# Sinkhorn's turning products as one of 128 stationary columns in place of four of 32

## The chip, the cores and the metric

One core of a Trainium2 chip runs the whole program. The metric is the device time of one execution in microseconds (us), as the median of several executions. The engines are TensorE (PE; PEld is its weight load), VectorE (DVE), ScalarE (ACT), GpSimd (POOL) and SyncE (SP), which issues DMAs.

## What is computed

Two layers over x (128 batches, 32 rows, 128 features). Layer 0 scales x by Sinkhorn's iteration and sends it through a routed feed-forward net; layer 1 is a GRU over the rows, then attention and a mixture of experts. The change lies in the first part alone:

```python
K = jnp.exp(-M / MU)
K = K / jnp.maximum(K.sum(axis=(-2, -1), keepdims=True), EPS)
u, v = r[..., None], 0
for _ in range(31):        # frozen once u has stopped moving
    v = c / jnp.maximum(jnp.einsum('bnm,bnk->bmk', K, u), EPS)
    u = r / jnp.maximum(jnp.einsum('bnm,bmk->bnk', K, v), EPS)
P = u * K * jnp.swapaxes(v, -2, -1)
```

K is 128 matrices of 32 x 128, u is one column of 32 and v one of 128 for each batch.

## The kernel before

`sinkhorn` keeps K in buf_a with the rows (n) of four batches on the partitions, and K transposed in buf_b with the features (m) on the partitions, already scaled by c. The 128 batches are cut into four groups h = 0 to 3 of 32 batches, so that the engines can work on different groups at the same time. Each group has a PSUM bank of its own, ps_g[h].

A round of the iteration has these steps for a group, each named after its function or operation:

- `to_columns(h)` (TensorE, L235): K times u. u stands block-diagonally in u_pad, 32 stationary columns a product. Eight products of 128 x 32 stationary and 128 moving columns, four to each of two accumulations; product j writes partitions 32j to 32j+31 of ps_v.
- den_v (ScalarE, L211): copies the 128 x 128 result from PSUM, with a bias that keeps it above zero.
- `turn(h)` (TensorE, L241): den_v has the features along its free axis. Products with den_v as the stationary operand and the 0/1 matrix `pick` (32 columns) as the moving one pick the wanted entries and put the features on the partitions. Four products, product q with columns 32q to 32q+31 of den_v, into partitions 32q to 32q+31 of ps_g[h], columns 256 to 287.
- `invert(h)` (VectorE, L329): the reciprocal, written block-diagonally to v_pad.
- `to_rows(h)` (TensorE, L249): K transposed times v, eight products like those of `to_columns`, into ps_u.
- `turn_back(h)` (L333), `inverse(h)` (L338) and `spread(h)` (L344) on VectorE: a transpose in blocks of 32, the reciprocal, and the next u_pad.

GpSimd keeps a history of u (L186 to L194), and ScalarE judges how far u has moved and keeps a history of v (L213 to L219). After the 31 rounds the history of the round at which the iteration would have stopped is read back.

The order on each engine is written out by hand in `one_round`; semaphores carry the rest. On TensorE it is: columns 0, columns 1, columns 2, turn 0, turn 1, columns 3, turn 2, rows 0, turn 3, rows 1, rows 2, rows 3. A turn waits for its den_v (semaphore v_den), rows wait for `invert` (v_ready), columns for `spread` of the round before (u_ready). TensorE's first round stands by itself, since there the rows also wait for the scaling of buf_b by c (L324); the other 30 run in a loop, two to a pass. SyncE fetches the weights of the next stages during the first rounds.

Every fp32 product is recorded as two passes, each with a weight load of its own.

Of the kernel before, what the change touches and what calls it, by code (L numbers as in the profile page):

```python
# [12 lines left out]
B, N, D = 128, 32, 128  # L13
# [47 lines left out]
def sinkhorn(nc, io, consts, K, KT, u_last, v_last, early, x_n):  # L61

    ident, ones = consts.ident, consts.ones
    NG, W, BW = GROUPS_S, T // GROUPS_S, TG * BG
    WIDE = 36
    with ExitStack() as ctx:
# [7 lines left out]
        pick = mem.sb("pick", [P, BG, BG, TI])  # L74
# [10 lines left out]
        den_v = mem.sb("den_v", [P, NG, D])  # L85
# [8 lines left out]
        stop = mem.sb("stop", [1, 1])  # L94
        stop_i = mem.sb("stop_i", [1, 1], I32)
        moved = mem.sb("moved", [P, ITERS, NG])
        ps_g = [mem.ps(f"ps_g{k}", [P, 512]) for k in range(NG)]
# [8 lines left out]
        v_mm, v_den, t_mm, v_ready, u_mm, turned, inv_done, u_kept = (  # L106
            mem.sem("s_" + n) for n in ("v_mm", "v_den", "t_mm", "v_ready", "u_mm", "turned", "inv_done", "u_kept"))
# [15 lines left out]
        with nc.Block() as block:  # L123

            @block.sync
            def _(sp):
                sp.dma_start(r_t[:], io["r_t"]).then_inc(s["cr_in"], 16)
                sp.dma_start(c_t[:], io["cond_t"]).then_inc(s["cr_in"], 16)
                for h in range(NG):
                    sp.dma_start(Kv[:, h * TG:(h + 1) * TG, :], xv[:, h * TG:(h + 1) * TG, :]).then_inc(x_in[h], 16)  # L130
                for h in range(NG):
                    sp.dma_start(of_group(KT[:], h), of_group(io["x_t"], h)).then_inc(xt_in[h], 16)

                sp.wait_ge(u_mm, 2 * NG)
                sp.dma_start(early.wx[:], io["gru_wx"].rearrange("(g p) d -> p g d", p=P)).then_inc(early.gru_in, 16)
                sp.dma_start(early.wh[:], io["gru_wh"].rearrange("(g p) d -> p g d", p=P)).then_inc(early.gru_in, 16)
                sp.dma_start(early.wp[:], io["gru_wp"]).then_inc(early.gru_in, 16)
                sp.dma_start(early.bias[:], io["gru_b"]).then_inc(early.gru_in, 16)
                sp.dma_start(early.h_in[:], io["cond_t"]).then_inc(early.gru_in, 16)
                sp.dma_start(early.up[:], io["up0_t"]).then_inc(early.ffn_in, 16)  # L140
                sp.dma_start(early.down[:], io["down0_t"].rearrange("(j p) d -> p j d", p=P)).then_inc(early.ffn_in, 16)
                sp.dma_start(x_n[:], io["x_nt"]).then_inc(early.ffn_in, 16)
                sp.dma_start(early.gate_w[:], io["gate_w0_t"]).then_inc(early.gate_in, 16)
                sp.dma_start(early.gate_b[:], io["gate_b0"].broadcast_to([P, 8])).then_inc(early.gate_in, 16)
# [77 lines left out]
            @block.tensor  # L222
            def _(pe):
                mm = nc.tensor.matmul
                pe.wait_ge(s["made"], 17)
                pe.wait_ge(s["ksums"], NG)
                mm(ps_s[:, 0:G], same_batch[:], ksum[:], start=True, stop=True).then_inc(s["sums_mm"], 1)
                pe.wait_ge(s["kinv_out"], 1)
                mm(ps_s[:, G:G + B], ones[:], kinv_row[:].rearrange("p c t -> p (c t)"), start=True, stop=True).then_inc(s["kinv_mm"], 1)

                def to_columns(h):
                    for i in range(TI):
                        for j in range(BG):
                            t = h * TG + j * TI + i
                            last = mm(ps_v[h][32 * j:32 * j + 32, :], u_pad[:, h, j, 32 * i:32 * i + 32], K[:, t * D:(t + 1) * D],  # L235
                                      start=i == 0, stop=i == TI - 1)
                    last.then_inc(v_mm, 1)

                def turn(h):
                    for q in range(4):  # L240
                        last = mm(ps_g[h][32 * q:32 * q + 32, 2 * D:2 * D + BW], den_v[:, h, 32 * q:32 * q + 32],  # L241
                                  pick[:].rearrange("p c j i -> p (c j i)"), start=True, stop=True)
                    last.then_inc(t_mm, 1)

                def to_rows(h):
                    for i in range(TI):
                        for c in range(BG):
                            b = c * G + h * TG + i * BG
                            last = mm(ps_u[h][32 * c:32 * c + 32, :], v_pad[:, h, c, 32 * i:32 * i + 32], KT[:, b * N:(b + BG) * N],  # L249
                                      start=i == 0, stop=i == TI - 1)  # L250
                    last.then_inc(u_mm, 1)

                def one_round(i, first):
                    pe.wait_ge(u_ready[0], i + 1)
                    to_columns(0)
                    pe.wait_ge(u_ready[1], i + 1)
                    to_columns(1)
                    pe.wait_ge(u_ready[2], i + 1)
                    to_columns(2)
                    pe.wait_ge(v_den, i + 1)  # L260
                    turn(0)
                    pe.wait_ge(v_den, i + 2)
                    turn(1)
                    pe.wait_ge(u_ready[3], i + 1)
                    to_columns(3)
                    pe.wait_ge(v_den, i + 3)
                    turn(2)
                    pe.wait_ge(v_ready, i + 1)
                    if first:
                        pe.wait_ge(s["kt_scaled"], 1)  # L270
                    to_rows(0)
                    pe.wait_ge(v_den, i + 4)
                    turn(3)
                    pe.wait_ge(v_ready, i + 2)
                    if first:
                        pe.wait_ge(s["kt_scaled"], 2)
                    to_rows(1)
                    pe.wait_ge(v_ready, i + 3)
                    if first:
                        pe.wait_ge(s["kt_scaled"], 3)  # L280
                    to_rows(2)
                    pe.wait_ge(v_ready, i + 4)
                    if first:
                        pe.wait_ge(s["kt_scaled"], 4)
                    to_rows(3)

                one_round(0, True)
                with nc.tensor.Fori(NG, NG * ITERS, 2 * NG) as i:
                    one_round(i, False)
                    one_round(i + NG, False)  # L290
# [1676 lines left out]
```

## Time and profile before

| | us |
|---|---|
| median of 3 runs (548.59 to 551.55) | 549.93 |
| the profiled execution's own time | 553.06 |
| its span in the trace | 551.3 |
| TensorE busy | 480.2 |
| VectorE busy | 371.9 |
| ScalarE busy | 319.2 |
| GpSimd busy | 182.3 |

The durations below come from the one profiled execution, which took 3.13 us more than the median. Sinkhorn runs from 16.8 to about 151 us of the span. The duration of a pass as shown is a latency with a modelled end: passes overlap, so the pace is read from where one group starts and where the next does. A start time is counted from the start of the span.

### The profile page before, as it was taken

The page shows a single profiled execution, that of the slowest core. Times are in us where ns is not written, and L with a number is a line of the kernel's source. Part 1 is how long each engine was busy: PE and PEld are TensorE (multiplying, and loading weights), DVE is VectorE, ACT ScalarE, POOL GpSimd, SP SyncE. Part 2 cuts the span into 40 slices and gives each one's busy share as a digit, 9 for nine tenths or more (in the row PEclk, how much of TensorE's full clock was granted, in tenths as well). Part 3 has the DMA queues.
Part 4 walks back from the last instruction along what each step waited for, and adds up shares of the span by engine and source line. Part 5 has one row for each costly group of instructions (what it writes and reads, how often), then busy time and mean ns, then how long its engine had stood idle before and what let it go on. Part 6 is the DMA issues. An engine that isn't in the chain of part 4 may idle for free. (4 is left out here: it accounts for less than half of the span.)

```text
span 551.3 us, 23767 instructions
## 1 busy us (share of the span) xinstructions
PE 480.2 (87%) x8992; PEld 395.2 (72%) x8992; DVE 371.9 (67%) x1329; ACT 319.2 (58%) x784; POOL 182.3 (33%) x445
## 2 busy tenths in 40 slices
PE   0799999999969989999999797799999840999994
PEld 0589999999847446666666595588888730999994
DVE  4778878878877656666575457368999875355552
ACT  4555555555546925564554535487888730777772
POOL 3244444444400000000000077223567663354553
PEclk9999999999979999999999977599999985999998
DMA  9261000000000367833300020000011122333330
GB/s 243 69 204 47 0 0 0 0 0 0 0 1 2 81 157 201 257 78 77 96 1 1 1 81 1 2 2 2 28 53 41 63 94 81 87 108 104 110 101 19
DMA packets 24190, 34.37 MB, mean 62 GB/s; under 512 B 3616, under 2 KB 17957, under 8 KB 23752
## 3 DMA queue, kind: packets, MB, share of 16 engines
q1 hardware_dynamic: 21360, 27.23, 17.9%
q0 software_dynamic: 2784, 6.56, 3.4%
q8 instruction: 25, 0.41, 0.3%
q14 instruction: 21, 0.17, 0.1%
HBM read 25.98 MB, written 8.26 MB: 62 GB/s over the span
## 5 line engine op out<-in xcount | busy, mean ns | idle before, releaser
L211 ACT ACTIVATE den_v<-ps_g,floor 128x128 f32<-128x128 f32 x124 | 45.5, 368 | 45.3 <-PE ps_g L235 41.3
L249 PE MATMUL ps_g<-buf_b,v_pad 128*32 128x128 f32 x1984 | 66.9, 274 | 1.9 <-DVE v_pad L329 1.4
L235 PE MATMUL ps_g<-buf_a,u_pad 128*32 128x128 f32 x1984 | 67.8, 278 | 0.3
L235 PEld LDWEIGHTS ps_g<-buf_a,u_pad 128*32 128x32 f32 x1984 | 53.8, 112 | 1.8 <-DVE u_pad L344 1.1
L1031 POOL MEMSET eps<- 128x1 f32 x1 | 0.1, 98 | 164.5 <-POOLq L572 164.5
L1773 POOL DMA_INDIRECT out<-yb,token_i x39 | 38.5, 987 | 47.7 <-DVE resid L1875 46.5
L249 PEld LDWEIGHTS ps_g<-buf_b,v_pad 128*32 128x32 f32 x1984 | 50.6, 110 | 2.8 <-DVE v_pad L329 2.1
L639 PE MATMUL ps_h<-buf_c,up 128*128 128x512 f32 x96 | 49.9, 616 | 0.3
L329 DVE RECIPROCAL v_pad<-ps_g 128x32 f32<-128x32 f32 x124 | 38.9, 334 | 14.0 <-PE ps_g L241 11.6
L1343 POOL TENSOR_TENSOR vb<-vn,row_mask 128x1024 f32<-128x1024 f32 x16 | 30.2, 1890 | 44.8 <-PE ps_o L1422 23.8
L1796 PE MATMUL m_h<-xT,w_near 128*128 128x128 f32 x312 | 42.4, 280 | 0.0
L1806 PE MATMUL m_y<-w,hid_t 128*128 x312 | 41.3, 275 | 0.1
L333 DVE STREAM_TRANSPOSE den_u<-ps_g 128x128 f32<-128x128 f32 x124 | 37.9, 306 | 4.0 <-PE ps_g L249 0.3
L193 POOL TENSOR_SCALAR held_u<-inv_u 128x8 f32<-128x8 f32 x124 | 24.3, 196 | 45.3 <-DVE inv_u L338 44.5
L1796 PEld LDWEIGHTS m_h<-xT,w_near 128*128 128x128 f32 x312 | 39.0, 196 | 0.2 <-ACT xT L1836 0.2
L1806 PEld LDWEIGHTS m_y<-w,hid_t 128*128 128x128 f32 x312 | 38.0, 192 | 0.3 <-issue 0.3
L1891 DVE TENSOR_TENSOR yb<-m_y,resid 128x128 f32<-128x128 f32 x39 | 11.4, 292 | 37.7 <-PE m_y L1806 37.7
L1336 POOL DMA_INDIRECT sorted_x<-rows,slot_i x32 | 31.4, 981 | 11.1 <-issue 7.9
L766 ACT ACTIVATE relu<-ps_h 128x512 f32<-128x512 f32 x48 | 28.2, 588 | 11.1 <-PE ps_h L639 11.1
L194 POOL TENSOR_TENSOR u_hist<-held_u,r_t 128x8 f32 x124 | 25.3, 204 | 22.4 <-POOL held_u L193 22.4
L241 PE MATMUL ps_g<-pick,den_v 128*32 128x32 f32 x992 | 31.3, 201 | 0.0
L649 PE MATMUL ps_y<-act,down 128*128 128x512 f32 x64 | 31.3, 593 | 0.0
(316 smaller groups left out, 1159.9 us busy)
## 6 DMA issues: line engine op xcount, KB each, us to landing
cw_b<-cw_d SPq DMA_DIRECT2D x16, 512.0 KB, 7.9
xt<-sorted_x SPq DMA_DIRECT2D x39, 136.0 KB, 2.2
w<-in_w SPq DMA_DIRECT2D x2, 2048.0 KB, 16.2
buf_a<-in_x SPq DMA_DIRECT2D x4, 512.0 KB, 6.6
buf_b<-in_x_t SPq DMA_DIRECT2D x4, 512.0 KB, 7.2
buf_d<-in_x_nt SPq DMA_DIRECT2D x1, 2048.0 KB, 8.8
sorted_x<-nobody SPq DMA_DIRECT2D x1, 1088.0 KB, 5.3
out<-yb,token_i POOLq DMA_INDIRECT x39, 2.5
```

What stands on the lines that cost most here:

```text
L211: fn(den_v[:, h, :], ps_v[h], ACT.Relu, bias=floor[:]).then_inc(v_den, 1)
L235: last = mm(ps_v[h][32 * j:32 * j + 32, :], u_pad[:, h, j, 32 * i:32 * i + 32], K[:, t * D:(t + 1) * D], start=i == 0, stop=i == TI - 1)
L241: last = mm(ps_g[h][32 * q:32 * q + 32, 2 * D:2 * D + BW], den_v[:, h, 32 * q:32 * q + 32], pick[:].rearrange("p c j i -> p (c j i)"), sta ...
L249: last = mm(ps_u[h][32 * c:32 * c + 32, :], v_pad[:, h, c, 32 * i:32 * i + 32], KT[:, b * N:(b + BG) * N], start=i == 0, stop=i == TI - 1)
L329: v.reciprocal(diagonal_v(h), ps_t[h]).then_inc(v_ready, 1)
L333: v.transpose(den_u[:, h, 0:D], ps_u[h]).then_inc(turned, 1)
L639: mm(ps_h[p % 2][:], up[:, j * P:(j + 1) * P], pt_n[:, q * W:(q + 1) * W], start=True, stop=True).then_inc(h_mm, 1)
L649: mm(ps_y[q % 2][:], down[:, ORDER[k], :], held(p), start=k == 0, stop=k == J - 1).then_inc(y_mm, 1)
L1336: g.indirect_dma_start(sorted_x, bass.IndirectOffsetOnAxis(ap=tables.slot_i[:, t:t + 1], axis=0), rows[:, t, :], None).then_inc(tables.sen ...
L1773: nc.gpsimd.indirect_dma_start(out, bass.IndirectOffsetOnAxis(ap=token_i[:, d:d + 1], axis=0), yb[:, k, :], None, bounds_check=T - 1, oob_ ...
L1796: last = mm(ps_h[d % 2][:, q * P:(q + 1) * P], w1_near[:, d % NEAR, q * P:(q + 1) * P], x_t[:, d % 2, :], start=True, stop=True)
L1806: last = mm(ps_y[d % 2][:, 0:D], hid_t[:, d % 2, q, :], w2[:, bass.ds(at + q * D, D)], start=q == 0, stop=q == Q - 1)
```

## The change

The four products of `turn` become one, whose stationary operand is the whole of den_v for the group (128 columns) and whose output is all 128 partitions. What is computed, the moving operand and the semaphore that the last product raises stay the same, as does everything else in the kernel.

```diff
                 def turn(h):
-                    for q in range(4):
-                        last = mm(ps_g[h][32 * q:32 * q + 32, 2 * D:2 * D + BW], den_v[:, h, 32 * q:32 * q + 32],
-                                  pick[:].rearrange("p c j i -> p (c j i)"), start=True, stop=True)
-                    last.then_inc(t_mm, 1)
+                    mm(ps_g[h][:, 2 * D:2 * D + BW], den_v[:, h, :], pick[:].rearrange("p c j i -> p (c j i)"),
+                       start=True, stop=True).then_inc(t_mm, 1)
```

## Rows read from the trace of the kernel before

**Rows 1.** The page: busy time of each engine, and TensorE's clock in 40 slices.

```profile
PE 480.2 (87%) x8992; PEld 395.2 (72%) x8992; DVE 371.9 (67%) x1329; ACT 319.2 (58%) x784; POOL 182.3 (33%) x445
...
PEclk9999999999979999999999977599999985999998
```

**Rows 2.** The page's costliest groups: busy us, mean ns, idle before and its releaser.

```profile
L249 PE MATMUL ps_g<-buf_b,v_pad 128*32 128x128 f32 x1984 | 66.9, 274 | 1.9 <-DVE v_pad L329 1.4
L235 PE MATMUL ps_g<-buf_a,u_pad 128*32 128x128 f32 x1984 | 67.8, 278 | 0.3
...
L241 PE MATMUL ps_g<-pick,den_v 128*32 128x32 f32 x992 | 31.3, 201 | 0.0
```

**Rows 3.** Timeline of TensorE's matmuls, one round: start us, length us, engine, line.

```profile
121.63 1.49 PE L235 MATMUL ps_g<-buf_a,u_pad 128*32 128x128 f32 x48
122.94 0.50 PE L241 MATMUL ps_g<-pick,den_v 128*32 128x32 f32 x16
123.26 0.62 PE L235 MATMUL ps_g<-buf_a,u_pad 128*32 128x128 f32 x16
123.70 0.24 PE L241 MATMUL ps_g<-pick,den_v 128*32 128x32 f32 x8
123.78 0.64 PE L249 MATMUL ps_g<-buf_b,v_pad 128*32 128x128 f32 x16
124.37 0.27 PE L241 MATMUL ps_g<-pick,den_v 128*32 128x32 f32 x8
124.45 1.50 PE L249 MATMUL ps_g<-buf_b,v_pad 128*32 128x128 f32 x48
125.77 0.40 PE L235 MATMUL ps_g<-buf_a,u_pad 128*32 128x128 f32 x8
```

**Rows 4.** Timeline of weight loads and ScalarE in the same round.

```profile
123.17 0.16 PEld L241 LDWEIGHTS ps_g<-pick,den_v 128*32 128x32 f32 x8
123.23 0.16 PEld L235 LDWEIGHTS ps_g<-buf_a,u_pad 128*32 128x32 f32 x8
...
124.37 0.16 PEld L241 LDWEIGHTS ps_g<-pick,den_v 128*32 128x32 f32 x8 [0.21 <-ACT den_v L211]
...
123.95 0.37 ACT L211 ACTIVATE den_v<-ps_g,floor 128x128 f32<-128x128 f32 x1 [0.39 <-PE ps_g L235]
```

**Rows 5.** Timeline of weight loads, 164.3 to 165.3 us, the feed-forward net's gate.

```profile
164.34 0.97 PEld L624 LDWEIGHTS ps_gz<-gate_w,buf_c 128*128 128x128 f32 x8
165.23 0.19 PEld L639 LDWEIGHTS ps_h<-buf_c,up 128*128 128x128 f32 x1
```

**Rows 6.** Timeline of weight loads, 442.7 to 445.3 us, attention.

```profile
443.95 0.30 PEld L1443 LDWEIGHTS ps_pt<-w_proj,o_t 128*128 128x128 f32 x2
444.17 0.31 PEld L1445 LDWEIGHTS ps_pt<-rows,ident 128*128 128x128 f32 x2
```

**Rows 7.** Timeline of matmuls, the same stretch of attention.

```profile
443.08 0.24 PE L1455 MATMUL ps_ss<-hot,every 128*128 128x32 bf16 x4
443.25 0.77 PE L1422 MATMUL ps_o<-vb,prob_t 128*32 128x36 f32 x64
```

**Rows 8.** Timeline of matmuls, 365.1 to 366.0 us, attention.

```profile
365.41 0.40 PE L1443 MATMUL ps_pt<-w_proj,o_t 128*128 128x136 f32 x2
365.64 0.40 PE L1445 MATMUL ps_pt<-rows,ident 128*128 x2
365.96 0.24 PE L1422 MATMUL ps_o<-vb,prob_t 128*32 128x36 f32 x4
```

**Rows 9.** Timeline of matmuls, end of the first round and start of the second.

```profile
24.19 0.65 PE L249 MATMUL ps_g<-buf_b,v_pad 128*32 128x128 f32 x16 [0.69 <-DVE v_pad L329]
24.90 2.17 PE L235 MATMUL ps_g<-buf_a,u_pad 128*32 128x128 f32 x48
```

**Rows 10.** Busy time of the engines in windows; the column before DMA is TensorE's clock.

```profile
300.00:350.00 50.00, 38.78 (x222) 33.37 (x230) 26.37 (x107) 25.03 (x54) 20.82 (x55) 0.81 0.07 23
...
400.00:450.00 50.00, 44.03 (x1252) 37.80 (x1251) 44.57 (x158) 36.78 (x88) 32.85 (x28) 1.00 0.16 57
```

## The prediction, made before the changed kernel was built

> **What bounds the kernel now.** I read the page's busy lines first: TensorE is busy 87% of the span, and the clock line stands at 9 (full) through slices 2 to 11, in which Sinkhorn runs [rows 1]. The costliest groups give the size of the stage: L235 and L249 have 1984 pass records each and L241, the line that the change touches, 992 [rows 2]. Over 31 rounds that is 64, 64 and 32 passes a round: 32 products of columns, 32 of rows and 16 of turning, since an fp32 product is two passes here.
>
> Then the timeline of TensorE over one round [rows 3]. Take 121.63 as zero: columns of groups 0 to 2 from 0, turn(0) at 1.31, columns of group 3 at 1.63, turn(2) at 2.07, rows of group 0 at 2.15, turn(3) at 2.74, rows of groups 1 to 3 at 2.82, next round at 4.14. Two things are to be seen. First, 48 passes take 1.31 us both times (121.63 to 122.94, 124.45 to 125.77): 27 ns each on average, which is one set of four passes in 0.109 us. The four products of a set go to four different 32-column strips and run beside one another. A round has 32 such sets, 32 x 0.109 = 3.49 us of its 4.14. Second, the remaining 0.65 us lies around the turns. Turn(1)'s first weight load starts at 123.17 and the weights of the next columns are loading at 123.23 [rows 4]; turn(3)'s starts at 124.37, with 0.21 us of idle load path ahead of it that ScalarE's den_v ended [rows 4]. The last set of columns(1) begins at 7 x 0.109 = 0.76, and turn(1) at 1.54: 0.78 later. The last set of columns(3) begins at 1.96, and turn(3) at 2.74: again 0.78. So the round's critical path is: columns 0 and 1, eviction by ScalarE, **turn(1)**, columns 3, eviction, **turn(3)**, rows 1 to 3. Each of those two turns costs 0.09 us on it (123.17 to 123.26, 124.37 to 124.45). Turn(0) and turn(2) lie in slack: 1.54 - 1.31 = 0.23 us before turn(1) may start, and 2.74 less the end of rows(0), which is 2.15 + 0.02 + 4 x 0.109 = 2.61, so 0.13 us. ScalarE is not the limit, its den_v takes 0.37 us four times a round [rows 4].
>
> **What the change removes.** Per turn, four products (eight passes, eight weight loads) become one (two and two): 24 passes less a round, 744 less in all. But the eight passes of today are two sets of four that run together, and a turn with its weights loaded ahead is over in 0.08 us (turn(2): 123.70, then rows(0) at 123.78 [rows 3]). What is removed is worth at most 0.09 us a turn.
>
> **What it adds, 1: wide weight loads.** A load of 32 columns becomes one of 128. Rows for that: eight loads of 128 fp32 columns at L624, whose products stream only 8 columns, start at 164.34, and the next group's at 165.23: 0.89 / 8 = 0.111 us each [rows 5]. Nothing hides in it: the load alone sets the pace. With no load ahead, L1443's two loads start at 443.95 and the next at 444.17 [rows 6]: 0.22 us until the second pass can stream. A turn is therefore 0.22 us of loads and then 32 columns, 0.027 us by the set's 0.109 for 128. Bounds: 0.11 if the first load were hidden, 0.22 if not; den_v or the switch below lies ahead of every turn but turn(1), and turn(1)'s first load can at best begin when turn(0)'s second has ended, so I take 0.22 for each.
>
> **What it adds, 2: a change of layout.** L235 and L249 use 32-column strips, the new turn the whole width. The kernel has this alternation in its attention stage. Whole to strips: L1455's four passes (8 columns, 0.24 us with the last's modelled tail of 0.166) start the last pass at 443.15, and the strips of L1422 begin at 443.25 [rows 6, 7]: 0.09 after its stream. Pairs of passes start every 0.23 us there (365.41, 365.64), so L1445's has streamed at 365.87; L1422 begins at 365.96 [rows 8]: 0.09. Strips to whole: L1422's 64 passes end, as modelled, at 444.02, each lasting 0.200, so the last starts at 443.82 and streams 36 columns (0.03); L1443's load starts at 443.95 [rows 6, 7]: 0.10. Where the layout stays, nothing of this is seen: L241 starts at 122.94, when the twelve sets before it are through [rows 3]. So a switch costs 0.09 us each way, with nothing streamed or loaded in it. A round gets three excursions (turn(0) with turn(1), turn(2), turn(3)), six switches. The bounds are 0 and 0.10; I take 0.09, as two of the three places have it.
>
> The Trainium skill speaks here against the change ("TensorEngine Tiling (Array Packing)", section Key Properties): changing the tiling mode, not just the tile, drains TensorE. It gives no time; the trace agrees, with 0.09 us. Without that rule the sum would be the 560 us of the second case below.
>
> **The new round**, from 0: columns 0 to 2 end at 1.31; switch, 1.40; turn(0)'s loads, 1.62; turn(1)'s den_v was ready at 1.54, its loads end at 1.84; it streams, 1.87; switch, 1.96; four sets, the first 0.024 longer as after a wait today (123.78 to 124.37 includes it), end 2.42, the last begun at 2.31; switch, 2.51; turn(2), 2.76; switch, 2.86; rows(0) end at 3.31; den_v(3) was ready at 2.31 + 0.78 = 3.09; switch, 3.41; turn(3), 3.66; switch, 3.75; twelve sets and 0.024, 5.08. **The round goes from 4.14 to 5.08 us.** As a check, all of it on TensorE: 3.49 + 4 x 0.22 + 3 x 0.027 + 6 x 0.09 + 3 x 0.024 = 5.07. No wait is left on the path. VectorE's reciprocal for rows(0) is due at 1.62 + 0.81 = 2.43 (today turn(0)'s last set starts 0.03 behind 122.94, and rows(0) 0.81 later, at 123.78), before 2.86; its spread for the next round keeps its 0.1 us of slack behind rows(0) and (1), which move as a block with turn(3).
>
> Rounds: 30 after the first. The second is longer today by its slow start (48 passes take 2.17 us as against 1.49 [rows 3, 9]), which is no wait at the turns, so it takes the cost in full like the rest: 30 x 0.945 = 28.4 us. The first is paced by the scaling of KT on VectorE (waits of 0.69 us for the reciprocal behind it [rows 9]); it takes between 0 and 0.9, I say 0.2. Everything behind Sinkhorn moves back as it is; its DMAs are landed long before. SP and POOL queues are passed by nothing. The sum against the profiled execution's own 553.06 us is 581.7; the median of the three runs is 3.1 lower, 549.93, so the forecast is **578.5 us**. This case's own range: 570 (the three switches into the turns hidden under the loads, 3 x 0.09 x 30 = 8.1 less) to 586 (0.13 for every switch, start to start as at L1443, instead of 0.09: 7.2 more).
>
> **Rivals.** (a) Loads, but no switch cost, because both layouts here use all 128 rows. For it: nothing in Sinkhorn's own rows shows a switch. Against: the three places above, two of them from the whole width to exactly this strip. Then turn(0)'s first load hides; turn(1) runs from 1.54 to 1.79, columns(3) start 0.16 late, turn(3) goes from 2.90 to 3.15, the round is 4.46: 30 x 0.32 = 9.7, so **560 us**. (b) The other side: TensorE is bound by how many passes it can issue. 160 passes in 4.14 us are 25.9 ns each; 24 fewer would save 0.62 us a round, 18.6 in all, so **531 us**. It decides if a wide pass costs one issue slot like a narrow one. Against: the passes of a set of four start together and the next set waits 0.109 us, which is the streaming of 128 columns; and L624's wide passes are 0.111 apart with 8 columns. The Trainium skill ("TensorE: Matmul & The Clock Gate", section Wait — 56ns, not 53.3ns?) states a floor of about 25 ns from start to start, however few columns; by that rule this rival would hold, and the average looks like it, but L624's pace does not follow it. (c) Both loads hide and no switch costs: the two turns on the path stream 2 x 0.027 instead of 0.09, 30 x 2 x 0.03 = 2 us less, **548 us**, no change. Against: den_v is what they load, and it is only just written. (d) TensorE's granted clock falls in Sinkhorn, as it does in 300 to 350 us (0.81) [rows 10], since six pauses a round are new. Against: 400 to 450 us, with the same alternation, has 1.00. A tenth of the stage at half clock costs some 15 us: **594 us**.
>
> **How the numbers follow.** Forecast case 0.80, (a) 0.09, (b) 0.03, (c) 0.03, (d) 0.05. The forecast case's own range leaves out more than 2 in 10 with the other cases, so the range reaches down to (a): 559 to 587. A measurement tells about 0.5% (2.7 us) from no change. Faster by more: (b), 0.03. Within it: (c), 0.03. Slower: 0.94.
>
> **What would show it.** Right, if in the profile after: L241 has 248 passes, its second load 0.11 after its first; between the last set of columns(2) and turn(0)'s load 0.2 us pass from start to start (0.109 and 0.09); from turn to next strips 0.12; a steady round of 5.08; ScalarE's den_v no longer ends a wait of L241; clock still 1.00. Wrong, if strips load while the wide product streams (a), if wide loads are 0.03 apart (b), or if the clock line drops below 9 in slices 2 to 12 (d).

## The result and the profile after

The changed kernel takes 578.6 us (median of 4 runs, 578.2 to 580.89) and the kernel before, on the same chip, 550.74 us (4 runs, 548.59 to 554.19): a ratio of 1.0508, with a 95% interval of 1.0445 to 1.0571. It is slower, by 27.9 us in the medians. The profiled executions are 25.1 us apart (553.06 and 578.2 us).

The page's busy lines and costliest groups of the kernel after, in the columns of [rows 1, 2]:

```profile
span 576.5 us, 22279 instructions
PE 507.1 (88%) x8248; PEld 410.6 (71%) x8248; DVE 374.5 (65%) x1329; ACT 318.7 (55%) x784; POOL 182.3 (32%) x445
...
PEclk9999999999998999999999997799999995799998
...
L247 PE MATMUL ps_g<-buf_b,v_pad 128*32 128x128 f32 x1984 | 67.4, 276 | 1.2 <-DVE v_pad L327 1.2
L235 PE MATMUL ps_g<-buf_a,u_pad 128*32 128x128 f32 x1984 | 67.9, 278 | 0.3
...
L240 PEld LDWEIGHTS ps_g<-pick,den_v 128*128 128x128 f32 x248 | 34.6, 189 | 18.5 <-issue 18.0
...
L240 PE MATMUL ps_g<-pick,den_v 128*128 128x32 f32 x248 | 44.9, 284 | 0.0
```

TensorE has 744 passes less (8992 to 8248) and is busy for 27 us longer. The turn's passes are down from 992 to 248, and yet their group is busy for 44.9 us where it was for 31.3 [rows 2]. The new entry is at the end of the load's line: the load path stood idle for 18.0 us ahead of L240, and what ended it is "issue", that is, nothing that the profile knows of. The line's own view counts them, beside what is left of the old wait:

```profile
L240 PEld LDWEIGHTS ps_g<-pick,den_v x248: 186/189/192, 18.6 to 177.6; 128*128 128x128 f32 x124
...
  issue: 18.0, 91
  ACT den_v L211: 0.5, 2
```

91 + 2 are three excursions a round in 31 rounds (an excursion is one stay in the wide layout between stretches of strips: turn(0) with turn(1), turn(2), turn(3)), of 0.2 us each: about half of it while the last set still streams, the rest with nothing in it. The wait for ScalarE's den_v ahead of turn(3), 0.21 us of idle load path in a round of before [rows 4], is gone: TensorE now comes later than den_v at all excursions but two.

One steady round, in the timeline of TensorE's matmuls (the columns of [rows 3]):

```profile
122.56 1.49 PE L235 MATMUL ps_g<-buf_a,u_pad 128*32 128x128 f32 x48
123.98 0.63 PE L240 MATMUL ps_g<-pick,den_v 128*128 128x32 f32 x4
124.55 0.64 PE L235 MATMUL ps_g<-buf_a,u_pad 128*32 128x128 f32 x16
125.12 0.41 PE L240 MATMUL ps_g<-pick,den_v 128*128 128x32 f32 x2
125.46 0.64 PE L247 MATMUL ps_g<-buf_b,v_pad 128*32 128x128 f32 x16
126.03 0.41 PE L240 MATMUL ps_g<-pick,den_v 128*128 128x32 f32 x2
126.37 1.52 PE L247 MATMUL ps_g<-buf_b,v_pad 128*32 128x128 f32 x48
127.70 1.49 PE L235 MATMUL ps_g<-buf_a,u_pad 128*32 128x128 f32 x48
```

The last line begins the next round. The round is 5.14 us (4.14 before [rows 3]). The twelve sets that took 1.31 us up to the next group's start now take 1.42 when a wide turn follows (122.56 to 123.98) and 1.33 when strips follow (126.37 to 127.70, a first set 0.02 longer included). A single wide turn takes 0.34 us up to the next strips (125.12 to 125.46, 126.03 to 126.37) and the pair 0.57.

Behind Sinkhorn nothing is changed. That part took 400.5 us in the profiled execution of before (150.8 to 551.3) and 397.2 in that of after (179.3 to 576.5). The granted clock of TensorE differs in and ahead of the attention stage:

```profile
302.00:352.00 50.00, 38.85 (x250) 33.03 (x249) 26.50 (x106) 23.30 (x51) 21.86 (x55) 0.79 0.07 23
352.00:402.00 50.00, 46.86 (x1303) 39.86 (x1302) 39.45 (x99) 38.92 (x88) 20.11 (x13) 0.94 0.04 13
```

```profile
330.00:380.00 50.00, 39.15 (x258) 33.54 (x257) 26.40 (x106) 23.83 (x52) 21.78 (x55) 0.83 0.07 23
380.00:430.00 50.00, 46.40 (x1316) 39.90 (x1315) 41.24 (x102) 40.41 (x92) 22.12 (x14) 1.00 0.04 13
```

The first two are the kernel before and the others the one after, 28 us on, in the windows' columns of [rows 10]: 0.79 and 0.94 of the full clock (2.4 GHz), then 0.83 and 1.00. The mean shares are 0.135 and 0.085 short of full over 100 us, so some 27 and 17 us of them passed at the lower level (1.2 GHz). In the other runs of this study the same unchanged part took 399 to 404 us, so this difference says nothing of the change. Sinkhorn's first product also came 0.84 us earlier in the execution of after (15.95 us of the span, before 16.79). Sinkhorn itself, from there to its end, is longer by 29.4 us; less 0.84 and 3.3 that leaves the 25.2 by which the two spans differ.

### The profile page after: what moved, and what is told of

Same layout as the page of the kernel before. It is cut to its first block and busy times, and to the rows that moved or that the text cites. A ratio compares the mean times of both kernels' runs of the same rounds, so it can differ in the third digit from the quotient of the medians.

```text
span 576.5 us, 22279 instructions
## 1 busy us (share of the span) xinstructions
PE 507.1 (88%) x8248; PEld 410.6 (71%) x8248; DVE 374.5 (65%) x1329; ACT 318.7 (55%) x784; POOL 182.3 (32%) x445
## 5 line engine op out<-in xcount | busy, mean ns | idle before, releaser
L327 DVE RECIPROCAL v_pad<-ps_g 128x32 f32<-128x32 f32 x124 | 40.0, 342 | 31.3 <-PE ps_g L240 31.3
L240 PEld LDWEIGHTS ps_g<-pick,den_v 128*128 128x128 f32 x248 | 34.6, 189 | 18.5 <-issue 18.0
L240 PE MATMUL ps_g<-pick,den_v 128*128 128x32 f32 x248 | 44.9, 284 | 0.0
```

Of the source, the lines that this page charges most:

```text
L240: mm(ps_g[h][:, 2 * D:2 * D + BW], den_v[:, h, :], pick[:].rearrange("p c j i -> p (c j i)"), start=True, stop=True).then_inc(t_mm, 1)
L327: v.reciprocal(diagonal_v(h), ps_t[h]).then_inc(v_ready, 1)
```

## Experiments

The steady round, read from the starts of columns(0) in each trace, is the measure here: from the fifth round on it repeats to within 0.003 us in the kernel before (4.138) and in the kernel after (5.144), and is not touched by what the clock does later. Single times are given beside a run of before on the same chip where they say something.

**One part at a time.** Three kernels make only some turns wide. In `turn` of the kernel before:

```diff
                 def turn(h):
+                    if h in (0, 1):     # (2,) in w2, (3,) in w3
+                        mm(ps_g[h][:, 2 * D:2 * D + BW], den_v[:, h, :], pick[:].rearrange("p c j i -> p (c j i)"),
+                           start=True, stop=True).then_inc(t_mm, 1)
+                        return
                     for q in range(4):
```

> Only turn(0) and turn(1) are wide, turn(2) and turn(3) stay in four strips. Theory (switches of the array's layout plus wide loads, less what slack hides): with the values that the changed kernel's trace shows (0.11 us from the end of a set to the wide load, 0.111 a wide load, 0.23 from the last wide load to the strips' first, the first set behind it 0.02 longer), columns(3) end 0.38 us later than in the kernel before, the steady round goes from 4.14 to 4.52 us, the time up by 11 us. Rival (only the loads cost): 0.16 a round, 4.30. Rival (the cost is a later result for VectorE, not TensorE's time): rows(0) is due with slack, so nearly no change.

> Only turn(2) is wide. Theory: columns(3) end at 2.07 of the round, the wide load starts at 2.18, the rows' load at 2.52, rows(0) end at 2.98, where turn(3) could start at 2.74 before: 0.13 of the 0.37 us are hidden by slack, the round is 4.14 + 0.24 = 4.38 us, the time up by 7 us. Rival (only the loads cost, first one hidden): the turn takes 0.14 in place of 0.06, all of it in slack, round 4.14 to 4.16.

> Only turn(3) is wide. Theory: the way into the wide layout hides in the wait for den_v(3), the loads and the way out do not: the rows start 0.26 later and their first set is 0.02 longer, round 4.14 + 0.28 = 4.42 us, the time up by 8 us. The three parts (0.38, 0.24, 0.28) sum to 0.90, 0.10 less than all turns wide cost (5.144 - 4.138 = 1.006), since with turn(2) wide the wait that hides turn(3)'s way in is gone. Rival (only the loads cost): 0.16, round 4.30. If the parts sum to 1.0, slack played no part.

Measured: 4.514, 4.37 and 4.41 or 4.45 us in turn (in w3 every second round has rows(0) 0.05 later behind turn(2)), so 0.38, 0.23 and, as a mean, 0.30 more than before. The forecasts from loads and switches were 0.38, 0.24 and 0.28; the rival of loads alone had 0.16 or nothing. The times, single ones, were 563.07, 558.34 and 559.42 us; the run of before beside them took 556.08, above all four of the comparison above, so the rounds and not these times are compared. TensorE's matmuls in a round of w2, and then its loads around turn(3) in w3:

```profile
110.12 0.62 PE L235 MATMUL ps_g<-buf_a,u_pad 128*32 128x128 f32 x16
110.68 0.41 PE L241 MATMUL ps_g<-pick,den_v 128*128 128x32 f32 x2
111.02 0.64 PE L253 MATMUL ps_g<-buf_b,v_pad 128*32 128x128 f32 x16
111.48 0.24 PE L245 MATMUL ps_g<-pick,den_v 128*32 128x32 f32 x8
111.54 1.50 PE L253 MATMUL ps_g<-buf_b,v_pad 128*32 128x128 f32 x48
```

```profile
112.20 0.30 PEld L241 LDWEIGHTS ps_g<-pick,den_v 128*128 128x128 f32 x2 [0.21 <-ACT den_v L211]
112.54 1.25 PEld L253 LDWEIGHTS ps_g<-buf_b,v_pad 128*32 128x32 f32 x48
```

These rows show what the slack does. In w2 turn(3) follows rows(0) without a wait (111.48, 0.46 us behind 111.02) and ahead of it the wait for den_v is used up. In w3 that wait is still there (0.21 us, ended by ScalarE), and the way into the wide layout hides in it: only 0.34 us behind the load (112.20 to 112.54) are paid in place of 0.08. The three parts sum to 0.90; all turns wide cost 1.006. The difference is one piece of slack counted twice: the wait ahead of turn(3) hides 0.13 us of turn(2)'s excursion in w2 and 0.11 us of turn(3)'s way in in w3, and with all turns wide it can hide only one of the two.

**The loads alone.** The changed kernel with each wide product issued twice:

```diff
-                    mm(ps_g[h][:, 2 * D:2 * D + BW], den_v[:, h, :], pick[:].rearrange("p c j i -> p (c j i)"),
-                       start=True, stop=True).then_inc(t_mm, 1)
+                    for k in range(2):
+                        last = mm(ps_g[h][:, 2 * D:2 * D + BW], den_v[:, h, :], pick[:].rearrange("p c j i -> p (c j i)"),
+                                  start=True, stop=True)
+                    last.then_inc(t_mm, 1)
```

> The changed kernel with each wide turn issued twice (same output, the semaphore on the second). No further switch. Theory: eight more wide loads a round of 0.111 each, all of them on TensorE's path: round 5.14 + 0.89 = 6.03 us, the time up by 27 us on the changed kernel. Rival (a wide pass costs an issue slot or its 0.027 us of streaming, and the whole price is in the switches): 0.2 a round, 5.35 us.

Measured: 6.038 us a round, 0.894 more for eight more wide passes: 0.112 us each. The time was 610.21 us. Its round begins:

```profile
141.97 1.49 PE L235 MATMUL ps_g<-buf_a,u_pad 128*32 128x128 f32 x48
143.39 1.08 PE L241 MATMUL ps_g<-pick,den_v 128*128 128x32 f32 x8
144.40 0.64 PE L235 MATMUL ps_g<-buf_a,u_pad 128*32 128x128 f32 x16
```

From 143.39 to 144.40 are 1.01 us with eight passes, where the changed kernel has 0.57 with four. The way in (141.97 to 143.39) is 1.42 us as there. A pass that streams 32 columns costs what its load of 128 costs, and the rival in which the price lies in the switches alone (5.35) is refuted.

**The switches alone.** The kernel before, with its turns in strips, and one more small product behind turn(1), turn(2) and turn(3), in all rounds but the first. `small` is a new bf16 tile of 128 x 128 ones; its product is one pass into a bank that nobody reads in these rounds:

```diff
+                def extra():
+                    mm(ps_s[:, 256:264], small[:], small[:, 0:8], start=True, stop=True)
...
                     turn(1)
+                    if not first:
+                        extra()
```

In extra_strip the product is `mm(ps_s[0:32, 256:264], small[:, 0:32], small[:, 0:8], ...)`.

> The kernel before, its turns in strips, with a small bf16 product of 128 stationary and 8 moving columns (one pass, into a bank that nobody reads) behind turn(1), turn(2) and turn(3) of every round but the first. It has the switches without the fp32 loads. Theory: each takes 0.11 in, some 0.03 for load and stream, 0.09 out: about 0.23 us more on the path behind turn(1) and turn(3), and 0.12 behind turn(2), where 0.13 is slack. Round 4.14 + 0.6 = 4.7 us, the time up by 18 us. Rival (no switch cost, the widths of loads alone): below 0.1 a round, 4.2 us, the time up by 2 us.

> The same extra product with 32 stationary columns in one strip: one more pass at the same three places, no switch. Both theories: 0.01 to 0.03 us each, at most 0.08 a round, round 4.14 to 4.22 us. It is the control of the run with 128 columns: the difference of the two is the switches. If it costs as much as that, the price is that of one more instruction and not of a switch.

Measured: 4.683 us a round with 128 columns and 4.200 with 32; 4.138 without. The times were 570.77 and 553.51 us beside 553.66 of before. First the one of 128 columns, then the one of 32:

```profile
114.87 0.50 PE L243 MATMUL ps_g<-pick,den_v 128*32 128x32 f32 x16
115.31 0.18 PE L248 MATMUL ps_sum<-small 128*128 128x8 bf16 x1
115.42 0.64 PE L237 MATMUL ps_g<-buf_a,u_pad 128*32 128x128 f32 x16
115.88 0.24 PE L243 MATMUL ps_g<-pick,den_v 128*32 128x32 f32 x8
116.06 0.18 PE L248 MATMUL ps_sum<-small 128*128 128x8 bf16 x1
116.16 0.64 PE L254 MATMUL ps_g<-buf_b,v_pad 128*32 128x128 f32 x16
```

```profile
107.10 0.17 PE L248 MATMUL ps_sum<-small 128*32 128x8 bf16 x1
107.11 0.62 PE L237 MATMUL ps_g<-buf_a,u_pad 128*32 128x128 f32 x16
107.55 0.25 PE L243 MATMUL ps_g<-pick,den_v 128*32 128x32 f32 x8
107.63 0.17 PE L248 MATMUL ps_sum<-small 128*32 128x8 bf16 x1
107.63 0.64 PE L254 MATMUL ps_g<-buf_b,v_pad 128*32 128x128 f32 x16
```

In a strip the product goes in with the others (107.10 and 107.11, 107.63 and 107.63). In the whole layout the same instruction, with 8 moving columns and one bf16 load, is 0.18 us behind the start of turn(2) (115.88 to 116.06) and keeps the rows away for 0.10 us more (116.16). So one more instruction is not the price, and three excursions cost 0.48 us a round even in today's slack, with not one wide fp32 load among them. The two runs also differ in the width of the bf16 load, 128 columns and 32. That can't be the price either: the four passes of L1455, with 128 stationary columns in bf16 and 32 down to 8 moving ones, start 0.025 us apart ([rows 7]: 0.24 less the last's 0.17, by three), loads included, so three such loads are at most 0.08 of the 0.48.

**Fewer switches.** The changed kernel with TensorE's order columns 0 to 3, turns 0 to 3, rows 0 to 3, and the same order with the turns in strips as its control:

```diff
                     to_columns(2)
-                    pe.wait_ge(v_den, i + 1)
-                    turn(0)
-                    pe.wait_ge(v_den, i + 2)
-                    turn(1)
                     pe.wait_ge(u_ready[3], i + 1)
                     to_columns(3)
-                    pe.wait_ge(v_den, i + 3)
-                    turn(2)
+                    for h in range(NG):
+                        pe.wait_ge(v_den, i + h + 1)
+                        turn(h)
...
                     to_rows(0)
-                    pe.wait_ge(v_den, i + 4)
-                    turn(3)
```

> The changed kernel with TensorE's order columns 0 to 3, turns 0 to 3, rows 0 to 3: one excursion a round in place of three, so two switches in place of six. Theory: columns end at 1.74, switch 1.86, eight loads of 0.111 without a gap (den_v(3) is ready at 2.42, before turn(3)'s first load at 2.52), last load 2.63, strips at 2.87, rows end at 4.63: round 4.63 to 4.75 us (the upper end if VectorE's order makes rows(3) wait), 0.4 to 0.5 less than the changed kernel's 5.144, the time down by 12 to 15 us on it. Rival (the loads are the price, or den_v's latency): grouping saves nothing or costs, 5.1 us or more.

> The same order with the turns in strips: the control of the wide one. Theory: no switch is saved, and turn(3) now waits for den_v(3) until 2.42, rows(0) for their reciprocal until 2.5 to 2.6: round 4.27 to 4.4 us, up by 0.13 to 0.25. So the same reordering gains with wide turns and loses with strips. Rival (the order is simply better): it falls below 4.14.

Measured, as means over the steady rounds: 4.88 us with wide turns (4.94 and 4.81 in turn) and 4.59 with strips. Both rounds are longer than was forecast (4.63 to 4.75 and 4.27 to 4.4). The times were 577.66 and 568.53 us beside 553.66; the wide one is hardly below the changed kernel's 578.6, because the part behind Sinkhorn took 403.2 us in this run and 397.2 in the profiled one of that kernel. Yet the sign is what the theory wants: the same reordering takes 0.27 us off the round with wide turns and adds 0.46 to it with strips, 0.7 us apart, of which four switches of 0.09 to 0.11 are 0.4. The rest goes, as far as the timelines show, to the wait for den_v(3), which the eight wide loads cover and the strips do not (TensorE idle for 0.3 us ahead of turn(3) in the run with strips); no run shows this share apart. What had been left out is in the loads of the wide one:

```profile
114.07 1.25 PEld L235 LDWEIGHTS ps_g<-buf_a,u_pad 128*32 128x32 f32 x48 [0.17 <-DVE u_pad L337]
115.49 0.38 PEld L235 LDWEIGHTS ps_g<-buf_a,u_pad 128*32 128x32 f32 x16 [0.17 <-DVE u_pad L337]
116.06 0.30 PEld L240 LDWEIGHTS ps_g<-pick,den_v 128*128 128x128 f32 x2 [0.20 <-ACT den_v L211]
```

Columns(0) and columns(3) now wait for VectorE's u. VectorE's `spread` for a group follows its rows by a transpose and a reciprocal, and that for group 3 ends behind columns(2). Grouping turned part of the switches that it saved into a wait on the other half of the cycle.

**A better order of the kernel before.** Its turns in strips, with columns(3) ahead of turn(1):

```diff
                     turn(0)
-                    pe.wait_ge(v_den, i + 2)
-                    turn(1)
                     pe.wait_ge(u_ready[3], i + 1)
                     to_columns(3)
+                    pe.wait_ge(v_den, i + 2)
+                    turn(1)
                     pe.wait_ge(v_den, i + 3)
                     turn(2)
```

> The kernel before, turns in strips, with columns(3) moved ahead of turn(1): columns 0, 1, 2, turn 0, columns 3, turn 1, turn 2, rows 0, turn 3, rows 1 to 3. It fills the 0.18 us in which TensorE waited for den_v(1). Theory (those waits are on the path, the rest is TensorE's streaming): columns(3) can start when their u is spread, at about 1.5 of the round in place of 1.63, and turn(3) comes at 2.63 in place of 2.74: round 4.03 us, the time down by 3 us (0.6%). Rival: the u of columns(3) comes no earlier than 1.6, or VectorE's order makes rows(1) wait: round 4.14, no change.

Measured: rounds of 4.04 and 4.06 us in turn, 0.09 less in the mean, and 550.38 us (11 runs) as against 553.3 (16 runs): a ratio of 0.9951, interval 0.9927 to 0.9976. That is a small gain but clear of the noise, and no other kernel here is faster than the one before. In its timeline columns(3) begin 0.17 us behind turn(0), where turn(1) used to wait:

```profile
104.60 0.24 PE L241 MATMUL ps_g<-pick,den_v 128*32 128x32 f32 x8
104.77 0.64 PE L235 MATMUL ps_g<-buf_a,u_pad 128*32 128x128 f32 x16
105.23 0.31 PE L241 MATMUL ps_g<-pick,den_v 128*32 128x32 f32 x16
105.44 0.64 PE L249 MATMUL ps_g<-buf_b,v_pad 128*32 128x128 f32 x16
```

The 0.17 us is the next limit: columns(3) start at 1.48 of the round (103.29 to 104.77), and the last `spread` of VectorE (L344) ahead of that starts at 104.53 and takes 0.19 us, so it ends at 104.72, 0.05 us ahead of columns(3). In the grouped run above, where the profile names `spread` as what columns(3) wait for, its row ends 0.06 ahead of them. So their u is most likely the wait here too, though the profile does not name it. An order in which the groups are spread evenly over the round, with the engines' orders rewritten to suit, was not tried.

## Why the prediction was right

**What bounds the round.** Right. That the evictions and then turn(1) and turn(3) are on the path, with 0.13 us of slack ahead of turn(3), is what w2 and w3 show, both within 0.02 us of a forecast worked out from it; and filling the first of the two waits gave 0.09 us back.

**Removed passes are worth nothing.** Right. 744 fewer passes did not shorten anything. The rival that counts issue slots (531 us) falls with the doubled turns: 0.112 us a wide pass. The floor of about 25 ns from start to start that the Trainium skill states ("TensorE: Matmul & The Clock Gate", section Wait — 56ns, not 53.3ns?) is what L1455's wide bf16 passes show, 0.025 us apart [rows 7], and a pass with a wide fp32 load is far above it. In strips it is no bound on single passes: the four of a set start 0.007 us apart. The rival in which all is hidden (548 us) falls with the doubled turns too.

**Wide loads.** 0.111 us was forecast from L624 [rows 5], and the doubled turns measure 0.112. That turn(1)'s first load could begin only when turn(0)'s second was over holds: the pair takes 0.57, the single 0.34, 0.23 apart for two loads.

**The switches.** Right in kind, a little small in size. The way out was put at 0.12 us from the last pass's start; with 0.34 us a single turn, less two loads of 0.111, it is 0.12. The profile's record of the last pass is no help there: it begins while that pass's load still runs. The way in was put at 0.09 us behind the end of the last set and is 0.11: 1.42 less 1.31. What was sized too small is this term, by the way L1422 before L1443 was read [rows 6, 7]. That reading started from the last pass of a set, and the working of the round counts sets from their first; the four passes of a set start one behind the other over 0.02 us. Counted from the last pass, the way in is 0.09 in the changed kernel too: that pass starts at 123.78 (122.56 + 1.49, less its 0.27), streams for 0.109, and the load follows at 123.98. The prediction's terms, added without rounding at each step, give 5.06 us and not the 5.08 or 5.07 that it has. Of the 0.08 that are missing to 5.144, the three ways in are 0.07; the rounding made the agreement look better than it is. That such a change of mode empties the engine, as the Trainium skill states ("TensorEngine Tiling (Array Packing)", section Key Properties), agrees with extra_whole: 0.48 us more a round than with the same product in a strip.

**The number of rounds.** All 30 rounds behind the first were to take the cost in full, and 29 did, with 0.99 to 1.01 us. The third did not: it was 4.99 us before and is 5.14 after, as long as all the others. The prediction took its cost as coming on top of whatever made that round longer. In the trace of before this is a pause inside the rows of groups 1 to 3:

```profile
32.55 1.26 PE L249 MATMUL ps_g<-buf_b,v_pad 128*32 128x128 f32 x36
34.17 0.63 PE L249 MATMUL ps_g<-buf_b,v_pad 128*32 128x128 f32 x12 [0.36 <-issue]
```

The rows go on 0.64 us late (36 passes at 27 ns end at 33.53), and the next columns start at 34.72, another 0.21 late. What ended the pause is "issue", nothing that the profile knows of, and the changed kernel has no such pause in its third round; why was not tried. The first round took 0.09 us more, not 0.2. It is no steady measure, though: with the doubled turns it took 11.1 us where it took 8.1 before. By the starts of columns(0) the stage is then longer by 29.4 us where the sum had 28.6: 29 x 0.06 more for the round, 0.79 less for the third round, 0.11 less for the first. The misses cancel in part, which is luck.

**From the stage to the time.** 28.6 us were to be added to 549.93, and the medians are 27.9 apart, with a run of before between 548.6 and 554.2: the agreement of 578.5 with 578.6 is closer than the terms deserve. The clock line stands at 9 in slices 2 to 12, in which the stage runs, and the mean granted clock of 20 to 170 us is 1.00, so rival (d) did not come, and rival (a), with loads alone, is refuted by extra_whole and by w2 (0.23 us more, where loads alone would have hidden).

## What to carry to other kernels

Four small products in four strips of the array that run together are one short set, not four instructions' worth of time; what a wide one must beat is the set's time (0.08 us for a turn here), with its loads hidden behind the set before. An fp32 product with 128 stationary columns and few moving ones costs its two loads (0.11 us each here), and if its neighbours work in strips, a switch in and a switch out as well. In these runs a switch cost about the same around one small bf16 pass as around two to eight wide fp32 ones, so keep one layout through a dense stretch, or put all the work of the other layout in one place and see which engine then is waited for. A part's price depends on the slack that the others leave: price a change of several parts as a whole round, not as a sum.

## What the runs showed of the hardware

- Between strips of 32 columns and the whole width TensorE stands empty for 0.11 us on the way in (counted from the end of the last set, sets being counted from their first pass; 0.09 from the last pass's) and about 0.09 on the way out, in the rounds of the changed kernel as in extra_whole. The profile has no name for it: it stands as idle time of the load path ended by "issue", 0.2 us at a time, overlapping the last set, or it is hidden in a wait that another engine ends.
- The price does not need a long stay: a bf16 product with 8 moving columns pays it too (0.10 us from its start to the rows' in extra_whole).
- One more small product in a strip, beside others in strips, costs 0.02 us (4.200 less 4.138, for three of them).
- The granted clock differed between two executions of unchanged code (0.94 and 1.00 in the same 50 us of attention), and the part behind Sinkhorn took 400.5 and 397.2 us; that the clock is the whole of this difference was not shown. Against that the length of a round inside the changed stage repeats to 0.003 us and is the better measure.
